# The second expert's rows loaded ahead of the sixth and seventh unit of weights in an attention and mixture-of-experts kernel

## What is computed

```
x = x + attention(layernorm(x), ctx; wq, wk, wv, wo)       # 375 context rows and 112 own rows as keys
t = layernorm(x)
logits = t @ gate_weight.T                                 # 8 experts, top 2, weights renormalised
for e in range(8):
    gate, up = split(t @ gate_up_proj[e].T)                # 512 -> 2 x 1024
    y = (silu(gate) * up) @ down_proj[e].T                 # 1024 -> 512
    out += combine_w[:, e] * y
x = x + out
```

## Time and profile before

| | us |
|---|---|
| median of 3 runs | 447.59 |
| lowest and highest | 446.64, 449.9 |
| the profiled execution: its time | 447.16 |
| its span, first to last instruction | 445.4 |
| PE busy in the span | 436.2 |
| DVE busy | 347.5 |
| ACT busy | 254.7 |
| POOL busy | 101.1 |

### The profile page before, as it was taken

How to read it: one execution, slowest core, us unless ns; L and a number is a source line. 1 busy time by engine, 2 the same in 40 slices (tenths; PEclk the granted TensorE clock), 3 DMA queues, 4 the chain that set the end, 5 groups by cost and what they waited for, 6 DMA issues and landing times.

```text
span 445.4 us, 7062 instructions
## 1 busy us (share of the span) xinstructions
PE 436.2 (98%) x2456; PEld 370.4 (83%) x2456; DVE 347.5 (78%) x657; ACT 254.7 (57%) x428; POOL 101.1 (23%) x131
## 2 busy tenths in 40 slices
PE   8999999999999999999999999999999999999994
PEld 6979888888887788888888888888888888888883
DVE  5867556755847579898898898988988898898863
ACT  4576435635537466666657566566656657566530
POOL 7071161371437253003003003003003002001111
PEclk9999999999999999999999999999999999999999
DMA  8997985324684375958757756856845856855411
GB/s 266 357 326 237 282 204 193 138 70 140 215 210 167 118 244 176 356 196 227 255 181 212 245 203 185 262 175 196 278 155 199 262 195 194 258 204 156 112 49 51
DMA packets 27775, 90.74 MB, mean 204 GB/s; under 512 B 2656, under 2 KB 8800, under 8 KB 27744
## 3 DMA queue, kind: packets, MB, share of 16 engines
q1 hardware_dynamic: 24288, 81.96, 56.4%
q0 software_dynamic: 3456, 8.40, 7.8%
HBM read 75.91 MB, written 14.45 MB: 203 GB/s over the span
## 4 chain that ended last, share of the span: by engine, by line
PE 88%; DVE 3%; DMA 3%; issue 2%; POOL 1%; ACT 1%; POOLq 0%; SPq 0%; DVEq 0%; ACTq 0%
PE PJ L469 12%; PE T L469 11%; PE PJ L470 6%; PE T L470 6%; PE PJ L269 3%; PE T L282 3%; PE PJ L271 3%; PE PJ L270 3%; PE SC L570 3%; PE SC L572 3%; PE SC L571 3%; PE SC L315 2%; PE SC L299 2%; PE SC L303 2%; PE SC L301 2%; PE R L570 2%
## 5 line engine op out<-in xcount | busy, mean ns | idle before, releaser
L1013 DVE TENSOR_TENSOR ul<-ng,uh 128x1536 fp32r<-128x1536 f32 x64 | 112.5, 1757 | 2.6 <-ACT uh L738 1.5
L738 ACT ACTIVATE uh<-ng 128x1536 fp32r<-128x1536 f32 x64 | 94.7, 1480 | 1.3 <-DMA ng<-in_units 1.3
L469 PE MATMUL PJ<-eb,uh 128*128 128x512 f32 x248 | 88.8, 398 | 0.2 <-DVE eb L1013 0.2
L469 PE MATMUL T<-eb,uh 128*128 128x512 f32 x248 | 88.7, 397 | 0.0
L470 PE MATMUL PJ<-eb,ul 128*128 128x256 f32 x248 | 69.6, 281 | 0.0
L470 PE MATMUL T<-eb,ul 128*128 128x256 f32 x248 | 69.6, 281 | 0.0
L1532 POOL DMA_INDIRECT out<-ys,yidx x14 | 24.8, 1768 | 172.2 <-ACT ys L936 170.0
L469 PEld LDWEIGHTS PJ<-eb,uh 128*128 128x128 f32 x248 | 46.6, 188 | 11.9 <-DVE eb L1013 0.7
L469 PEld LDWEIGHTS T<-eb,uh 128*128 128x128 f32 x248 | 46.6, 188 | 11.2
L470 PEld LDWEIGHTS T<-eb,ul 128*128 128x128 f32 x248 | 46.8, 189 | 1.3
L470 PEld LDWEIGHTS PJ<-eb,ul 128*128 128x128 f32 x248 | 46.7, 188 | 1.2
(11 more groups left out here) (252 smaller groups left out, 926.2 us busy)
## 6 DMA issues: line engine op xcount, KB each, us to landing
ng<-in_units SPq DMA_DIRECT2D x64, 768.0 KB, 4.4
vs<-in_ctxn SPq DMA_DIRECT2D x8, 768.0 KB, 5.0
kTs<-in_ctxT SPq DMA_DIRECT2D x8, 750.0 KB, 7.4
slots<-zero SPq DMA_DIRECT2D x8, 514.0 KB, 12.4
xe<-slots SPq DMA_DIRECT2D x8, 514.0 KB, 4.5
wTs<-in_weights SPq DMA_DIRECT2D x8, 512.0 KB, 7.5
xt<-in_x SPq DMA_DIRECT2D x7, 256.0 KB, 15.1
out<-xt SPq DMA_DIRECT2D x7, 256.0 KB, 4.3
```

Of the source, the lines that this page charges most:

```text
L469: nc.tensor.matmul(o[:, :].rearrange("p (h s) -> p h s", h=2), wh, both[:, k, :, :], start=k == 0, stop=False)
L738: nc.scalar.activation(o, i, ACT.Copy).then_inc(s, 1)
L1013: v.tensor_tensor(o, whole, hi.bitcast(F32), ALU.subtract).then_inc(s, 1)
```

## The change

SyncE's queue is reordered. `load_ahead` now first loads the fifth unit (number 4) alone. The waits for the stores, the scatters and `early_T`, and the load of the second expert's rows, follow at once; the sixth and seventh unit (numbers 5 and 6) are issued behind these rows, and `load_xe(0, 0)` behind them. No instruction is added or removed on another engine, and every semaphore keeps its counts.

```
-            load_ahead(0, range(LG))
+
+            load_ahead(0, range(1))
             sp.wait_ge(x2_out, 16 * (NB - 1) + 16 * 2)
             for a in range(2):
                 sp.wait_ge(scattered[a], sent(a, PAIRS))
             sp.wait_ge(early_T, 2)
             load_xe(ER, 1)
+            load_ahead(0, range(1, LG))
             load_xe(0, 0)
```

## The result

| | before | after |
|---|---|---|
| median, 11 executions each | 448.73 us | 452.2 us |
| lowest and highest | 446.64, 450.33 | 451.16, 455.49 |
| ratio, with its 95% interval | | 1.0086 (1.0068 to 1.0105) |
| the profiled execution, time and span | 447.16, 445.4 | 451.5, 449.7 |

The change costs 0.86% or 3.9 us (3.1 to 4.7). The forecast for the pause alone was 5.5 us; the direction and the mechanism are as forecast, the size is not. One execution of the kernel before, among those that e1 to e4 are compared with, took 2461.82 us and is left out of the ratios as slow.

What follows compares the result with a forecast made beforehand. PE, 98% busy, was taken to bound the kernel. Unit 5 landing at 181.6 plus 5.5 us of path puts PE at 187.1 against 181.5, a 5.5 us pause: 447.59 + 5.5 = 453.1 us, range 451.2 to 456.0.

Steps and rivals of the forecast that it cites:

- the pause alone: PE waits before unit 3's down product because unit 5 lands late: 5.5 us, clock held; chance 0.48.
- what bounds the kernel: PE, busy 98% of the span; in the expert part any new idle stretch goes straight into the end.
- the path from landing to PE: From unit 5's landing through ACT and DVE to h_ok for unit 3: 5.38 us, PE about 0.1 later.
- The slack: Of ACT's 6.9 us delay, the first 1.5 are free: h_ok was up at 180.04 and used at 181.53.
- the cover of units 6 and 7: Both land before the delayed ACT wants them, unit 6 with 1.8 us to spare; unit 7's 1.34 wait goes.
- the term X: Issue of the second expert's rows on SyncE after the last scatter lands: 175.1, bounded by 173.4 and 175.4.
- the term L - X: Unit 5's landing counted from the issue of the rows: 6.5 us, bounded by 6.1 and 7.5.
- its own signs: Prediction wrong if unit 5 lands before 180 or after 183.5, PE stops again within two units, or the clock falls.
- Rival 2: Freed DMA engines let the last scatter land sooner, rows at 173.4: pause 3.5 us, time 451.1; chance 0.11.
- Rival 1: PE's pause also drops the clock, slowing matmuls behind it: 1.6 us more, 454.7; chance 0.33.
- Rival 3: Loads share the DMA engines instead of queueing, unit 5 lands at 184.0: pause 8.0 us, 455.6; chance 0.06.
- Rival 4: Change does nothing, as the scatter is done when SyncE gets there: 447.6; no effect or faster, chance 0.02.

Runs made afterwards that it cites:

- e1: Changed kernel, but unit 5 stays ahead of the scatter wait and only unit 6 goes behind the second expert's rows; ratio 0.9996 to the kernel before.
- e4: Changed kernel, but unit 5 goes last, behind both row loads and unit 6; ratio 1.0168 to the kernel before.
- e2: Changed kernel, but unit 6 stays ahead of the scatter wait and only unit 5 goes behind the second expert's rows; ratio 1.0134 to the kernel before.
- e3: Changed kernel, but units 5 and 6 go ahead of the second expert's rows, still behind the scatter wait; ratio 1.004 to the kernel before.
- e6: Load order of e2, with the first pass of PE's expert loop written out and no filling matmuls; median 456.46 us, ratio 1.0134 to the kernel before.

## Why the prediction was right and where it was off

**Right: what bounds the kernel, and that PE's idle time counts in full.** The last result moved by the pause, 2.86 and 2.86. That the two agree to the hundredth is luck: measured from L521, the last result of the changed kernel is 3.2 behind the second trace of the kernel before (278.51 against 275.27). The stretch from unit 3's down product to the last result is 256.3 to 256.9 in the six traces whose clock holds, so single traces are compared to about 0.5 us, the prices of the clock among them.

**Right: the place and the path from landing to PE.** The prediction had 5.38 from the landing to h_ok and about 0.1 more. From the start of unit 5's copy to PE's down product it is 5.44 in the changed kernel, 5.43 in e2, e3 and e4, and 5.44 in the second trace: five landings spread over 6 us, one path. The down product itself comes 2.9 to 3.0 late in the two traces of the changed kernel. The slack was 1.5 in the prediction and is 1.4.

**Right: the cover of units 6 and 7.** Neither makes ACT wait, there is no second pause, and the 1.34 wait for unit 7 vanishes without a gain.

**Off: the term X, the issue of the rows.** Forecast 175.1, measured 173.28, which is the lower bound less 0.1. The step that failed is the reading of the last 3 us before the landing: the DMA engines are 1% busy there, and I took this as a sign that nothing had been in the scatter's way. It only says that its data had moved by then. I also counted unit 6's issue, "nearly 10 us before", from the landing; from the scatter's start at 168.51 it is 2.6, and unit 6 landed 5.1 after its issue, at 171.0, so its transfer reached 2.5 into the scatter. e1 and e2 settle which load counts: without unit 6 ahead, 172.99; with unit 6 ahead and unit 5 not, 175.55. The comparison that I set aside, the same scatter of the pair before (4.7), was the right one: it takes 4.6 after the change.

The traces also show what unit 6 does. The profile counts the DMA packets of each queue; the four scatters make 320, 80 each, on GpSimd's queue:

| us | before: scatters | before: SyncE's loads | after: scatters | after: SyncE's loads |
|---|---|---|---|---|
| 162 to 166 | 80 | 51 | 79 | 0 |
| 166 to 169 | 0 | 66 | 104 | 0 |
| 169 to 173 | 240 | 78 | 137 | 0 |

Before, no packet of the second, third or fourth scatter moves from 166 to 169, while unit 6's do; then all three go together. After, they are spread over the whole stretch. In both kernels the last packet moves between 172 and 173, so the last scatter's data is delayed by less than 1 us. But before, three landings follow one another, at 172.5, 174.1 and 175.2 (starts at 164.19, 167.00 and 168.51, plus 8.3, 7.1 and 6.7); after, the third is at 171.3 and the last at 173.1. The 3 us of idle DMA engines before the last landing are the time of these landings. That the last one stands behind the other two is argued from this order; why landings come 1.1 to 1.8 apart stays open.

**Off: the term L - X, the landing of unit 5 behind the rows.** Forecast 6.5 with 6.1 as the lower bound, measured 178.93 - 173.28 = 5.65. The load takes 5.2 from its issue, and 5.3 and 5.2 in e2 and the second trace. The rows take 3.8 in the second trace, not 4.0, and the unit lands 1.9 behind them, not 2.1: these are the 0.4 by which even the lower bound was too high. The other 0.4 is my step from the bound to 6.5. The bound was worked out from two row loads, scaled by size; they move pieces of 2 KB and a unit moves pieces of 6 KB, and whether that is why the scaling fails was not tried.

The two terms are 1.8 and 0.9, together 2.7 of pause that did not come: 5.5 - 2.7 = 2.8. Both errors have one sign. Unit 5 landed at 178.93, outside the 180 to 183.5 that the prediction gave itself, and the clock fell in some executions; by its own signs the prediction was wrong on these two points. That the median of 452.2 lies within 0.9 us of the forecast 453.1 is luck: the median of the kernel before came out at 448.73 and not at the 447.59 from which the forecast started, which gives back 1.1 of the 2.7, and the measured cost is 0.6 to 1.0 more than the pause.

**The rivals.** Rival 2 (freed DMA engines bring everything forward) holds in full as to the scatter's landing, and in its time: it gave a loss of 3.5 us and a result within 1%, and 3.9 was measured; I gave it 0.11. That its time fits too is partly the clock: the pause alone came out shorter still, 2.9, by the second term. Rival 1 (the clock) occurs in a part of the executions, with about the price that I had taken: 1.1 here, 1.0 to 1.7 in the experiments against 1.6. But its condition was misread. I took from the tail that the clock holds through 5.1 us without a matmul and falls only at the end of such a pause; it fell 2.7 us into the pause of e2 and 2.9 into that of e4, and after a pause of 3.0 in the second trace. Rival 3 (sharing) falls with e3 and e4: unit 5 lands by its place in the queue. Rival 4 falls with the new wait.

## What to carry to other kernels

A load moved behind a wait must be priced at its first consumer, and through the order of that engine's program: here ACT, whose late copy of unit 5 also holds back the work for unit 3 that stands behind it, with 5.4 us of path from the copy to PE. When a load is moved away from a stretch, look for what else was using the DMA engines there, also when the stretch just before the landing looks idle; here the same transfer in a stretch without the neighbour (4.7 us) foretold its time after the change (4.6). A transfer that is late for one engine is worth bringing forward only if its consumer waits: the rows came 2.1 us earlier and nobody had been waiting for them.

## What the runs showed of the hardware beyond the forecast

- A 768 KB load by SyncE issued 2.6 us before the last of four indirect scatters by GpSimd (165.88 and 168.51) lengthens that scatter from 4.6 to 6.7 us, though 2.9 us of nearly idle DMA engines lie ahead of its landing. The third scatter goes from 4.3 to 7.1. From 166 to 169 us only the load's packets move.
- The granted clock fell 2.7 us into a pause of 4.7 without a matmul (e2, from the end of the transposition at 182.04) and 2.9 us into one of 6.5 (e4), and in the second trace of the changed kernel 1.4 us behind the end of one of 2.7, when PE had already run matmuls again. It came back 4.8 us behind the end of the pause in e2, 3.3 in e4 and 4.4 in e6, at a price of 1.0 to 1.7 us. At the end of the kernel it held for 5.1 us without a matmul. 40 small matmuls in the pause kept it up, and brought back 1.4 us.
- From the end of GpSimd's last issue to the end of the span it took 3.6 to 3.8 us in two of ten traces and 4.9 to 5.5 in the others, with the same program in that stretch. A span read from one trace carries this 1.5 us.
